# Moving the layer norm's application from VectorE to ScalarE in a two-layer adaLN transformer kernel

## The reference, cut to what matters

```python
def _layernorm(x, axis=-1, eps=1e-05):
    m = jnp.mean(x, axis=axis, keepdims=True)
    v = jnp.var(x, axis=axis, keepdims=True)
    return (x - m) / jnp.sqrt(v + eps)

x = L0_attn_x                                  # (2, 2048, 128)
h = _layernorm(x) * (1 + ca) + sa              # layer 0, norm before attention
x = x + ga * _L0_attn_ref(h, Wq, Wk, Wv)       # causal (k=1), RoPE, one head of 128
h = _layernorm(x) * (1 + cb) + sb              # layer 0, norm before the FFN
x = x + gb * _L0_ffn_ref(h, ...)               # FP4-quantised inputs, silu(gate) * up, down; 352 wide
h = _layernorm(x) * (1 + ca) + sa              # layer 1
x = x + ga * _L1_attn_ref(h, qk, ov)           # causal
h = _layernorm(x) * (1 + cb) + sb
x = x + gb * _L1_ffn_ref(h, ...)               # router, 8 experts of 64 (top 2), shared expert of 128
```

## Time and profile before

| what | value |
|---|---|
| time, median of 3 runs | 739.22 us (738.45 to 745.1) |
| the profiled execution's own time | 745.29 us |
| its span, first to last instruction | 743.5 us |
| TensorE busy | 637.9 us (86%), mean granted clock 0.929 |
| VectorE busy | 511.9 us (69%) |
| ScalarE busy | 319.8 us (43%) |
| GpSimd busy | 222.5 us (30%) |
| chain that ended last | PE 66%, DVE 21%, ACT 4%, POOL 4%, issue 4% |

### The profile page before, as it was taken

How to read it: one execution, slowest core, us unless ns; L and a number is a source line. 1 busy time by engine, 2 the same in 40 slices (tenths; PEclk the granted TensorE clock), 3 DMA queues, 4 the chain that set the end, 5 groups by cost and what they waited for, 6 DMA issues and landing times.

```text
span 743.5 us, 10881 instructions
## 1 busy us (share of the span) xinstructions
PE 637.9 (86%) x3739; PEld 504.5 (68%) x3747; DVE 511.9 (69%) x1465; ACT 319.8 (43%) x644; POOL 222.5 (30%) x225
## 2 busy tenths in 40 slices
PE   5398799989777999978989998968889996899997
PEld 4256577867656778775668786846677785676674
DVE  5946679685679667736669778596865754876665
ACT  1123344444334554533344444523455453555453
POOL 3323646253554211003455435254421102000000
PEclk9559999999979999999989999988999998799999
DMA  8300000000000000000000000000000000001001
GB/s 260 108 1 0 2 1 1 1 1 1 0 1 1 1 1 1 1 1 0 2 1 1 2 1 1 2 0 1 1 0 1 1 1 1 1 15 29 15 16 43
DMA packets 12078, 9.64 MB, mean 13 GB/s; under 512 B 1708, under 2 KB 10744, under 8 KB 12024
## 3 DMA queue, kind: packets, MB, share of 16 engines
q1 hardware_dynamic: 12024, 8.94, 4.0%
HBM read 6.84 MB, written 2.10 MB: 12 GB/s over the span
## 4 chain that ended last, share of the span: by engine, by line
PE 66%; DVE 21%; ACT 4%; POOL 4%; issue 4%; DMA 1%; SPq 0%; POOLq 0%; ACTq 0%
PE ps L771 14%; PE ps L641 12%; PE ps L749 8%; PE ps L601 5%; DVE xn L1312 5%; PE ps L914 4%; PE ps L916 4%; PE ps L915 3%; PE ps L659 2%; PE ps L794 2%; PE ps L795 2%; PE ps L595 2%; PE ps L810 2%; DVE row_max L1349 1%; DVE xn L1219 1%
## 5 line engine op out<-in xcount | busy, mean ns | idle before, releaser
L1075 ACT ACTIVATE probsT<-ps 128x512 f32<-128x512 f32 (+3 forms) x160 | 85.2, 533 | 181.9 <-PE ps L749 181.9
L771 PE MATMUL ps<-v_sb,probsT 128*128 128x129 f32 (+1 forms) x1148 | 158.6, 281 | 3.7 <-ACT probsT L1077 3.7
L771 PEld LDWEIGHTS ps<-v_sb,probsT 128*128 128x128 f32 (+1 forms) x1148 | 142.6, 192 | 11.1 <-ACT probsT L1077 5.7
L1349 DVE TENSOR_REDUCE row_max<-ps 128x1 f32<-128x512 f32 (+2 forms) x144 | 87.7, 619 | 49.2 <-PE ps L641 18.5
L749 PE MATMUL ps<-ident,probs 128*128 128x128 f32 (+1 forms) x574 | 94.3, 282 | 17.5 <-ACT hT L1021 6.1
L749 PEld LDWEIGHTS ps<-ident,probs 128*128 128x128 f32 (+1 forms) x574 | 66.2, 141 | 50.1 <-issue 46.5
L1049 ACT ACTIVATE probs<-ps,neg_max 128x512 f32<-128x512 f32 (+7 forms) x158 | 92.8, 618 | 16.7 <-DVE neg_max L1356 16.0
L473 POOL TENSOR_TENSOR rstd<-veps,half 128x4 f32<-128x4 f32 x34 | 34.2, 1012 | 154.1 <-DVE veps L1203 153.9
L501 POOL TENSOR_TENSOR hq<-ha,hp 128x352 f32<-128x352 f32 x32 | 29.9, 933 | 135.1 <-DVE hp L1390 135.1
L641 PE MATMUL ps<-k_high,q_high 128*128 128x512 f32 (+4 forms) x112 | 46.7, 417 | 0.2 <-ACT probs L997 0.2
L1312 DVE TENSOR_SCALAR xn<-x_sb,mv,rstd 128x128 f32<-128x128 f32 x112 | 41.4, 435 | 2.2 <-POOL rstd L473 2.2
(11 more groups left out here) (238 smaller groups left out, 1374.6 us busy)
## 6 DMA issues: line engine op xcount, KB each, us to landing
out<-x_sb SPq DMA_DIRECT2D x8, 256.0 KB, 2.3
x_sb<-in_L_attn_x SPq DMA_DIRECT2D x2, 512.0 KB, 5.3
hT_all<-in_L_wmod SPq DMA_DIRECT2D x2, 384.0 KB
rope_cos<-table_cos SPq DMA_DIRECT2D x1, 768.0 KB, 7.8
rope_sin<-table_sin SPq DMA_DIRECT2D x1, 768.0 KB, 9.7
rope_cos<-table_cos SPq DMA_DIRECT2D x1, 256.0 KB, 4.1
rope_sin<-table_sin SPq DMA_DIRECT2D x1, 256.0 KB, 5.1
moe_raw<-in_L_ffn_expert_gate_w SPq DMA_DIRECT2D x1, 256.0 KB, 3.1
```

The source lines that it names most:

```text
L771: mm = pe.matmul(bank(OUT_AT, 0, V_W), probsT[0:size, n % 4, k * P:(k + 1) * P], v_sb[0:size, j, :], start=(c == 0 and k == 0), stop=(c == ...
L1075: ins = act.activation(probsT[:, n % 4, 0:full], bank(TURN, 0, full), ACT.Copy)
L1349: ins = dve.tensor_reduce(dst, ps[:, start:start + width], AX.X, ALU.max, negate=single)
```

## The change

Step 3 goes to ScalarE, as xn = rstd * x + shift with shift = -mean * rstd (an Identity activation whose scale and bias are columns of SBUF). GpSimd forms the shift: it now runs three instructions for a group instead of one, and the third waits for the second. The copies `carry_wait` are left out on VectorE, and so are the two calls of `first_normalise` and those of `normalise_in_slot`. ScalarE calls them where `c == 0`, behind `copy_hq` and ahead of `exp(s, c + 2)`. The semaphore `rstd_ready` becomes GpSimd's own, and `norm_ready` (one for each kind) is what ScalarE waits for.

```diff
@@ gpsimd
-            def rsqrt_at(kind, n):
+            def scale_and_shift(kind, n):
                 pool.wait_ge(var_ready[kind], n)
-                pool.tensor_tensor(rstd[:, kind, :], veps[:, kind, :], half[:], ALU.pow).then_inc(rstd_ready[kind], 1)
+                pool.tensor_scalar(minus_mean[:, kind, :], mv[:, kind, :, 0], -1.0, None, ALU.mult)
+                pool.tensor_tensor(rstd[:, kind, :], veps[:, kind, :], half[:], ALU.pow).then_inc(rstd_ready, 1)
+                powers[0] += 1
+                pool.wait_ge(rstd_ready, powers[0])
+                pool.tensor_tensor(shift[:, kind, :], minus_mean[:, kind, :], rstd[:, kind, :],
+                                   ALU.mult).then_inc(norm_ready[kind], 1)
@@ scalar
+            def normalise_group(kind, batch, g):
+                for t in range(GROUP):
+                    ins = act.activation(xn[:, g, t * P:(t + 1) * P], x_sb[:, batch * TILES + g * GROUP + t, :], ACT.Identity,
+                                         scale=rstd[:, kind, t:t + 1], bias=shift[:, kind, t:t + 1])
+                return ins
+
+            def first_normalise(b, batch, g):
+                act.wait_ge(norm_ready[2], (b + 1) * GROUPS + g + 1)
+                normalise_group(2, batch, g).then_inc(xn0_ready, 1)
+
+            first_normalise(-1, 0, 0)
             act.wait_ge(turned, 1)
             act.activation(hT[:, 0:BANK], bank(TURN), ACT.Identity, scale=mod_col[:, 0, 1:2],
                            bias=mod_col[:, 0, 0:1]).then_inc(copied, 1)
+            first_normalise(-1, 0, 1)
...
+                def normalise(kind, n, g):
+                    act.wait_ge(norm_ready[kind], b * NORM_GROUPS[kind] + n + 1)
+                    return normalise_group(kind, b, g)
...
                         if c == 0 and ffn_tile(s, DOWN_LAG) is not None:
                             copy_hq(s - DOWN_LAG)
+                        if c == 0:
+                            normalise_in_slot(s)
+                            if s in (NEXT_SLOT - 1, NEXT_SLOT + 1):
+                                first_normalise(b, BATCH - 1 - b, int(s > NEXT_SLOT))
                         if c + 2 < n:
                             exp(s, c + 2)
+                normalise_in_slot(SLOTS + 1)
                 put_v_at(0, (b + 1) * 2 * GROUPS)
@@ vector
-            def carry_wait():
-                dve.tensor_copy(tick[:], ones[:, 0:1])
-
             def send_statistics(kind, link):
-                carry_wait()
                 for k in range(GROUP):
...
                     for c in range(1, following):
                         maximum(s + 1, c)
-                    normalise_in_slot(s)
-                    if s in (NEXT_SLOT - 1, NEXT_SLOT + 1):
-                        first_normalise(b, BATCH - 1 - b, int(s > NEXT_SLOT))
                     if ffn_tile(s, FFN_LAG) is not None:
                         quantise_h(s - FFN_LAG)
```

More of the change, by code:

```diff
@@ L212, in build @@
         rstd = sb("rstd", [P, 3, GROUP])
+        minus_mean = sb("minus_mean", [P, 3, GROUP])
+        shift = sb("shift", [P, 3, GROUP])
         tick = sb("tick", [P, 1])
@@ L327, in build @@
         var_ready = [sem(f"var_ready_{k}") for k in range(3)]
-        rstd_ready = [sem(f"rstd_ready_{k}") for k in range(3)]
+        rstd_ready = sem("rstd_ready")
+        norm_ready = [sem(f"norm_ready_{k}") for k in range(3)]
         xn1_ready = sem("xn1_ready")
@@ L468, in _ @@
             pool.tensor_copy(ident_b[:], ident[:]).then_inc(consts, 1)
-            def rsqrt_at(kind, n):
+            powers = [0]
+            def scale_and_shift(kind, n):
                 pool.wait_ge(var_ready[kind], n)
-                pool.tensor_tensor(rstd[:, kind, :], veps[:, kind, :], half[:], ALU.pow).then_inc(rstd_ready[kind], 1)
-            rsqrt_at(2, 1)
-            rsqrt_at(2, 2)
+                pool.tensor_scalar(minus_mean[:, kind, :], mv[:, kind, :, 0], -1.0, None, ALU.mult)
[4 more added lines that the diff above has]
+                                   ALU.mult).then_inc(norm_ready[kind], 1)
+            scale_and_shift(2, 1)
+            scale_and_shift(2, 2)
             pool.wait_ge(fp4_scaled, 1)
@@ L485, in rsqrt @@
                 def rsqrt(kind, n):
-                    rsqrt_at(kind, b * NORM_GROUPS[kind] + n + 1)
+                    scale_and_shift(kind, b * NORM_GROUPS[kind] + n + 1)
                 def modulate_1(g):
@@ L1025, in copy_group, with normalise_in_slot @@
                     act.activation(hT_group[:], bank(TURN), ACT.Identity, **args).then_inc(copied, 1)
+                def normalise(kind, n, g):
+                    act.wait_ge(norm_ready[kind], b * NORM_GROUPS[kind] + n + 1)
+                    return normalise_group(kind, b, g)
+                def normalise_in_slot(s):
+                    at = lambda first: group_at(s, first + 1)
+                    if early_group(s, NORM0_SLOT + 1) is not None:
+                        normalise(2, early_group(s, NORM0_SLOT + 1), early_group(s, NORM0_SLOT + 1)).then_inc(xn0_ready, 1)
+                    if at(NORM1_SLOT) is not None:
+                        normalise(0, at(NORM1_SLOT), at(NORM1_SLOT)).then_inc(xn1_ready, 1)
+                    if at(NORM2_SLOT) is not None:
+                        normalise(1, at(NORM2_SLOT), at(NORM2_SLOT)).then_inc(xn_ready, 1)
+                    if at(NORM3_SLOT + 1) is not None:
+                        normalise(0, GROUPS + at(NORM3_SLOT + 1), at(NORM3_SLOT + 1)).then_inc(xn_ready, 1)
                 def put_v(g, n):
@@ L1214, in first_statistics @@
                 send_statistics(2, link)
[L1216 to L1221, removed]
             def first_rotate(b, which, link):
@@ L1248, in _ @@
             last.then_inc(setup_dve, 1)
-            first_normalise(-1, 0, 0)
             dve.wait_ge(xn0_ready, 1)
@@ L1261, in _ @@
             dve.tensor_scalar(fp4_abs, fp4_abs, 1.0, ROUND, ALU.max, ALU.mult).then_inc(fp4_scaled, 1)
-            first_normalise(-1, 0, 1)
             dve.wait_ge(rope_first_loaded, 32)
@@ L1306, in statistics @@
                         send_statistics(kind, link)
[L1308 to L1326, removed]
                 def rotate(g, which, banks):
@@ L1473, in _ @@
                         take_logits(group_at(s, LOGIT_SLOT))
-                normalise_in_slot(SLOTS + 1)
                 first_maximum(b)
```

## The result

The changed kernel takes 780.57 us in the median of 4 runs (774.83 to 787.63), beside 739.38 us of the kernel before (738.45 to 745.1). The ratio is 1.051, with a 95% interval from 1.045 to 1.056: slower by 41 us, where the prediction had 760 and a range up to 778, so that the median lies 2.6 us above the range. The profiled execution was the shortest of the four, 774.83 us.

A forecast was written before the change was run, and what follows sets the result against it. TensorE was taken as the bound (66% of the chain). Two batches +20, setup -2.9 and copies -1 gave +16 us, the clock +5: +21 on the 739.22 us median, so 760 us, range 746 to 778.

The forecast's parts named there:

- the clock: TensorE's clock falls behind half of six new standstills in slots 8, 24 and 29 of both batches: +5 us.
- the mechanism: In slots with a third chunk, ScalarE's normalisation delays the exponential for which TensorE waits; +8 to +37 us, chance 0.70.
- slot 16: No third chunk; xn on ScalarE lets VectorE start the FFN's quantisation earlier, quantised input 3.0 us earlier: -3.0 us.
- the setup: VectorE's four instructions leave; GpSimd's FP4 work ends at 30.5 and TensorE can start then, not at 33.45: -2.9 us.
- Prices: ScalarE's xn instruction 445 ns, a group 1.45 us; GpSimd's two new instructions 0.2 us each, `norm_ready` after 1.4 us.
- the clock takes more: Rival: every new standstill drops the clock, or GpSimd's new instructions run near their high bound; 779 us, chance 0.13.
- Slots 20 and 21: No third chunk; the group stands ahead of the second chunk's copy, mostly a wait for xn before: +0.6 us together.
- VectorE's relief: Rival: relieving VectorE decides, the waits for xn go and the kernel is faster; 714 us at best, chance 0.07.
- Slots 12 and 24: ScalarE waits for GpSimd's shift, then normalises ahead of the exponential: net +2.1 us in slot 12, +3.1 in slot 24.
- The end of a batch: Behind the last slot, GpSimd's step grows by 0.4 us and xn by 0.33, with nothing beside them: +0.7 us.
- the stalls cancel within 1%: Rival: low bounds for both prices and no loss of clock give +3 us, 742 us; chance 0.10.
- What would show it: Signs in the changed profile: ScalarE's idle time for the shift, TensorE's waits for exponential and xn, clock, lengths of slots.

The follow-up runs named there:

- second profile of before: The kernel before, not edited, profiled once more: 741.2 us.
- the order of the two statements: The changed kernel with ScalarE's normalisation behind the third chunk's exponential instead of ahead of it: 748.27 us, ratio 1.009.
- wait alone: The kernel before plus GpSimd's two new instructions; VectorE still normalises, ScalarE only waits for the shift at the change's place: 755.17 us, ratio 1.016.
- work alone: The kernel before plus four unread ScalarE instructions a group at the change's place, waiting for no other engine: 766.13 us, ratio 1.031.
- the kernel by slot: The changed kernel with ScalarE normalising only in the setup and slots 1, 3, 4 and 16, VectorE elsewhere: 734.31 us, ratio 0.989.
- choosing slot by slot: The changed kernel, ScalarE normalising in slots 1, 3, 4, 8, 12 and 16 only, behind the third chunk's exponential: 728.67 us, ratio 0.984.
- the longer chain alone: The kernel before plus GpSimd's negated mean and shift, for which VectorE waits, ScalarE left alone: median 750.11 us, ratio 1.009 from three of seven executions.

## Why the prediction was right in kind and too small in size

The forecast was +21 us: +16 of standing, setup and copies included, and +5 for the clock. Against the second profile of before, the changed kernel has +22.1 of standing and +11.5 of busy time in its first profile, +20.4 and +19.4 in its second. So the mechanism was right, and two terms were too small: the clock by 6.5 to 14.4 us, the standing by 4.4 to 6.1, of which about 2.5 are slot 16 and 1.7 the setup.

- **The mechanism** is shown: the exponential behind the normalisation in ScalarE's queue. TensorE's standstills there, in the changed kernel's timeline, are 2.78 us in slot 8 (2.7 forecast), 4.36 in slot 12 (4.1), 3.59 in slot 24 (3.7), 1.17 in slot 25 (1.35) and 2.93 in slot 29 (2.75). Both the order of the two statements and the wait alone and work alone confirm it.
- **Prices.** One ScalarE instruction takes 484 ns, not 445, and a group 1.65 us, not 1.45: it lies 123 ns above the exponential with one column, not the 84 that I carried over. How much of that is the second column and how much the other function and source, no run here tells. By the Trainium skill, "ScalarE: Activation LUTs", section "What ACT_TABLE_LOAD costs", I had worked out 479 ns and 1.64 us, and the trace agrees with that. GpSimd takes 0.23, 1.03 and 0.20 us, ready after 1.5 (1.4 forecast); its bound of 3.0 wasn't touched.
- **The clock**, the term that fell short by most. I had +5 us: half of six standstills at 1.7 us, on a base of one profile. TensorE's busy time grew by 11.5 us in one profile and 19.4 in the other, against the second profile of before. Slot 24 alone holds 1.9 and 2.7 us of it in each batch, beyond 3.4 more of standing. So the rival "the clock takes more" with its 779 came nearer than the forecast's own number, though not for the whole of its reason: not every new standstill is followed by a lower clock, and a part of the miss is standing. Its other road, GpSimd's instructions near 3.0 us, is out. What decides whether a standstill costs clock stays open.
- **The setup.** -2.9 was expected and 1.8 measured between profiles, of which only 0.4 belong to the move to ScalarE. The copies account for 0.5 and slots 1 and 2 for 0.2; the rest is the difference between executions (the kernel by slot has the same setup and finishes slot 0 later by 0.45). The step that failed is the last one of that working. GpSimd's FP4 work did end where I had it, at 30.7 us (30.5 forecast), but VectorE's rotation, which TensorE waits for too, was not free by then. It began 4.8 us earlier, and its next three instructions then lay beside that FP4 work and took 7.1 us together instead of 1.8, so that TensorE went on at 32.5, 1.0 us earlier and not 2.9. What was gone from xn had come back in the rotation; that GpSimd's work beside them is the reason is argued from the place, not tested (changed kernel; 0.69, 0.43 and 0.69 us before):

```profile
24.14 1.95 DVE L1265 TENSOR_TENSOR rope_t<-rope_t 128x512 f32<-128x512 f32 x1
26.12 2.65 DVE L1266 CAST k_high<-rope_t 128x512 fp32r<-128x512 f32 x1
28.57 2.15 POOL L493 TENSOR_TENSOR probs<-probs,fp_s 128x1120 f32<-128x1120 f32 x1
28.81 2.47 DVE L1267 TENSOR_TENSOR k_low<-rope_t,k_high 128x512 fp32r<-128x512 f32 x1
...
32.53 2.71 PE L634 MATMUL ps<-ident,probs 128*128 128x128 f32 x12 [4.69 <-DVE rope_t L1262]
```

- **Slots 20 and 21**, put at +0.6 together: slots 20 to 23 came to +2.9 and +0.5 in the first batch's two profiles and to +1.3 and -1.1 in the second's, and most of that spread is the clock. One step is missing in my working: in slot 20, too, ScalarE stands for the shift, and TensorE for the copy behind it, 2.31 us, which the wait for xn of 1.79 us that was there before pays for in part:

```profile
232.58 1.65 ACT L983 ACTIVATE xn<-x_sb,shift,rstd 128x128 f32<-128x128 f32 x4 [2.53 <-POOL shift L482]
...
234.13 0.26 ACT L1115 ACTIVATE probsT<-ps 128x128 f32<-128x128 f32 x1
...
234.44 0.49 PE L781 MATMUL ps<-v_sb,probsT 128*128 128x129 f32 x2 [2.31 <-ACT probsT L1115]
```

- **Slot 16** gained 2.1 us, not 3.0. The wait for xn went from 3.60 to 1.91, but the wait for the quantised input grew from 2.05 to 3.04 instead of falling. GpSimd begins to modulate that group 4.36 us behind its own start in the slot before the change (202.01 - 197.65) and 4.29 behind it after (199.80 - 195.51): xn of that group is no earlier on ScalarE, and my 3.0 had the quantised input come earlier by VectorE's relief alone.
- **Slots 12 and 24**, in standing alone: +2.3 (and 0.6 more in slot 13) against +2.1, and +3.4 against +3.1.
- **The end of a batch**: +0.7 forecast; with slots 1, 3 and 4 +0.4; the stretch from there to slot 5 of the second batch is +0.9 and +1.5.
- **The rivals.** The move does help (slots 8, 12 and 16 in the later experiments), where TensorE waits for nothing that stands behind it on ScalarE. Whether by VectorE's relief or by xn from ScalarE, no run tells apart. That the stalls cancel within 1% is out.
- **What would show it:** ScalarE's idle time for the shift is 2.41 us in slot 24 and 1.60 in slot 8 as said, 1.32 rather than 2.5 in slot 12 (of the 2.7 us that I had there 1.45 were the first group's own work, so my own working gives 1.3), and 2.53 in slot 20, which I had not named. The wait for the exponential is 32.8 and not 15 to 25: I had named only part of what my own list of slots adds up to. The wait for xn stayed at 13.5, not under 5; it keeps 2.3 us in the setup, 1.9 in slot 16 and 3.3 at the end of each batch. Slots 16 to 19 are 2.1 us shorter in the first batch and 3.1 in the second (3 forecast). The third scores behind slot 24's start come 3.8 us later, not 4.4 (the +3.7 worked out for slot 24 was the right number). The mean clock fell under 0.929, as said, but barely, to 0.926 and 0.914, and a third execution of the changed kernel (780.5 us) has 0.936: by itself it shows little.

## What to carry to other kernels

An engine at 43% may still have no room at the place that matters: before moving work, look at what stands directly behind it in that engine's queue and who waits for that. Work that waits for another engine belongs behind what is wanted at once; here the exchange of two statements was worth some 32 us, and choosing slot by slot turned 5% slower into 1.6% faster. Price the clock apart, from TensorE's busy time at the same instruction count and from two profiles of the same kernel, since a single profile can differ by more than the term that you work out from it.

## What the runs showed of the hardware

- The same standstill of 2.8 us was followed by a granted clock of 1.00 in one execution and 0.57 in another of the same kernel (slot 8). A new standstill is a chance of slower matmuls, not a fixed price. What decides between them stays open.
- Most slots repeat to 0.03 us between kernels where the clock is the same; where it isn't, they differ often in steps of 1.3 to 1.7 us (slot 10: +1.3 to +1.7 in four kernels that don't touch it). Such steps can go either way: slots 17 to 19 of the second batch are 2.7 us shorter with the wait alone, the work alone and the longer chain alone.
- Leaving out 98 copies whose durations add up to 15.0 us took only 4.4 us off VectorE's busy time (511.9 to 507.5): they overlap their neighbours, so their listed mean of 154 ns is no price for leaving them out.
